# A transformer block on one core: another order for the first stretch, K in halves, V five beats later

## The reference

```python
def _tc_rmsnorm(x, t, gw, gb, bw, bb):
    g = (t @ gw.T + gb)[:, None, :]
    b = (t @ bw.T + bb)[:, None, :]
    return g * x * jax.lax.rsqrt(jnp.mean(x * x, axis=-1, keepdims=True) + EPS) + b

def _L0_cond_ref(x, t, ...):
    # 16 heads of 8 features; hidden width 512
    x = x + _attention(_tc_rmsnorm(x, t, g1w, g1b, b1w, b1b), Wq, Wk, Wv, Wo)
    return x + _swiglu(_tc_rmsnorm(x, t, g2w, g2b, b2w, b2b), gate_w, hid_w, out_w)

x = x + _L0_cond_ref(x, cond_256, ...)
```

## Time and profile before

| | us |
|---|---|
| median of the timed runs | 257.89 |
| the profiled execution | 257.42 |
| its span, first to last instruction | 255.6 |
| TensorE busy | 221.2 |
| VectorE busy | 202.9 |
| ScalarE busy | 163.3 |
| GpSimd busy | 111.9 |

### The profile page before, as it was taken

One profiled execution on the slowest core, in us unless ns is written; L12 is line 12 of the kernel. 1 busy time (PEld: TensorE's weight loads), 2 busy tenths in 40 slices (PEclk: granted clock), 3 DMA queues, 4 the chain that ended last, 5 costly groups with the idle time before them and its releaser, 6 DMA issues.

```text
span 255.6 us, 8235 instructions
## 1 busy us (share of the span) xinstructions
PE 221.2 (87%) x3048; PEld 177.9 (70%) x3048; DVE 202.9 (79%) x490; ACT 163.3 (64%) x352; POOL 111.9 (44%) x183
## 2 busy tenths in 40 slices
PE   2436777879989999899989999999999999899894
PEld 2314545547667868786878877887888778687894
DVE  4646966897899889889988998899888997565673
ACT  5354658676876686669766777567757655666430
POOL 8323852597265254625381516252623232323320
PEclk9995579999999999999999999999999999999998
DMA  5866601530261026100540045004500000000001
GB/s 162 345 169 147 185 4 28 152 85 3 64 166 27 26 64 164 47 23 19 140 124 0 27 112 152 10 27 114 156 6 26 4 26 3 23 3 24 22 21 44
DMA packets 18819, 18.79 MB, mean 74 GB/s; under 512 B 3644, under 2 KB 17980, under 8 KB 18652
## 3 DMA queue, kind: packets, MB, share of 16 engines
q1 hardware_dynamic: 18252, 17.80, 24.7%
q10 hardware_dynamic: 528, 0.46, 0.8%
HBM read 3.22 MB, written 2.10 MB: 21 GB/s over the span
## 4 chain that ended last, share of the span: by engine, by line
PE 45%; issue 24%; POOL 16%; DVE 9%; ACT 4%; ACTq 1%; POOLq 0%; DVEq 0%
PE proj L489 7%; PE pv L427 6%; PE ffn L320 5%; PE ffn L322 3%; PE ffn L321 3%; PE score L410 3%; DVE nmax L756 3%; POOL inv L923 3%; PE raw L383 3%; POOL qp L915 2%; PE tok L442 2%; POOL xn_lo L936 2%; POOL kp L915 2%; POOL xs L929 2%; PE proj L349 2%
## 5 line engine op out<-in xcount | busy, mean ns | idle before, releaser
L756 DVE TENSOR_REDUCE nmax<-raw 128x8 f32<-128x1024 f32 x61 | 74.2, 1216 | 3.0 <-PE raw L383 2.9
L597 ACT ACTIVATE p_s<-score 128x1024 f32<-128x1024 f32 x64 | 65.5, 1023 | 16.1 <-PE score L410 14.9
L427 PE MATMUL pv<-p_s,va 128*32 128x128 f32 x1024 | 41.7, 280 | 1.8 <-ACT xn L615 1.1
L320 PE MATMUL ffn<-xn_hi,ffn_hi 128*128 128x256 f32 x106 | 34.8, 328 | 1.2 <-POOL xn_lo L936 1.2
L626 ACT ACTIVATE th<-ffn 128x256 f32<-128x256 f32 x53 | 20.3, 384 | 19.6 <-PE ffn L322 19.6
L489 PE MATMUL proj<-ffn_out_s,hT 128*128 128x128 f32 x240 | 31.6, 275 | 0.0
L813 DVE SCALAR_TENSOR_TENSOR gated<-th,ffn 128x256 f32<-128x256 f32 x53 | 22.0, 415 | 12.1 <-ACT th L626 11.7
L427 PEld LDWEIGHTS pv<-p_s,va 128*32 128x32 f32 x1024 | 24.7, 109 | 9.2 <-issue 4.0
L936 POOL TENSOR_TENSOR xn_lo<-xn,xn_hi 128x128 fp32r<-128x128 f32 x32 | 14.7, 460 | 34.6 <-DVE xn_hi L804 34.6
L322 PE MATMUL ffn<-xn_hi,ffn_lo 128*128 128x256 f32 x106 | 29.7, 280 | 0.0
L321 PE MATMUL ffn<-xn_lo,ffn_hi 128*128 128x256 f32 x106 | 29.6, 279 | 0.0
(11 more groups left out here) (130 smaller groups left out, 456.0 us busy)
## 6 DMA issues: line engine op xcount, KB each, us to landing
ks<-kp SPq DMA_DIRECT2D x48, 128.0 KB, 2.4
qs<-qp SPq DMA_DIRECT2D x45, 128.0 KB, 2.5
out_y<-x_s SPq DMA_DIRECT2D x16, 128.0 KB, 1.8
x_s<-in_x SPq DMA_DIRECT2D x1, 1536.0 KB, 10.9
qs<-shift SPq DMA_DIRECT2D x64, 4.0 KB
x_s<-in_x SPq DMA_DIRECT2D x2, 256.0 KB, 3.6
ffn_in_s<-in_ffn_in_w SPq DMA_DIRECT2D x1, 512.0 KB, 6.7
qs<-qp ACTq DMA_DIRECT2D x3, 128.0 KB, 3.7
```

What stands on the lines that cost most here:

```text
L320: pe.matmul(dst, w_hi, v_hi, start=True, stop=False)
L427: mm = pe.matmul(pv[VW * j:VW * j + VW, (t % 2) * L:(t % 2 + 1) * L], va[vbuf(g)][:, t // 2, at:at + VW], p_s[:, (BEATS * g + t) % PBUF, p ...
L597: act.activation(p_s[:, n % PBUF, :], score[:], ACT.Exp, scale=SCALE).then_inc(s_exp, 1)
L756: dve.tensor_reduce(heads[:, :, t % 2, :], raw_dst(g, t)[:].rearrange("l (e j m) -> l e j m", e=HALVES, j=HQ), AX.X, ALU.max, negate=True) ...
```

## The change

- K of group 0 is computed in two halves of 256 columns (`first_key`), each behind its own half of `xn_lo`; `qk_lo` is made on GpSimd ahead of the second `a_inv`.
- On ScalarE the two last normalisations of group 1 stand ahead of the issue of the high queries' DMAs. The mean of group 2 and the zero fill of `va[1]` stand ahead of the middle part of Q of group 1.
- The cast to `ffn_hi` moves from beat 4 to the place behind `a_hi(1, 1)` on VectorE, and `ffn_lo` from beat 5 to behind `a_lo(1, 1)` on GpSimd.
- VectorE takes the first two maxima between the rests of K and Q of group 1. Six instead of seven raw scores stand ahead of beat 0; raw 6 and 7 come in beats 0 and 1, and raw 0 of group 1 at the end of beat 1. Only raw 1 and 3 use the bank `score`.
- V of group 0 moves behind the first score, and V of group g from beat 8g - 7 to 8g - 2. Its waits, and those of K and of the FFN's output, are adapted.
- `c_tr2` stands behind the next beat's `c_score` for beats below 10.

```diff
-    VALUE, KEY, QUERY = -7, -14, -13
+    VALUE, KEY, QUERY = -2, -14, -13
...
-            return score if g == 0 and t % 2 and t < BEATS - 1 else raw
+            return score if g == 0 and t % 2 and t < HQ else raw
...
+        def raws_in(T):
+            if T < 2:
+                return [(0, BEATS - 2 + T)]
+            return due(T, RAW, BEATS)
...                                       (a_values on TensorE)
-                elif g == 1:
-                    pe.wait_ge(s_va, 1)
                 else:
-                    pe.wait_ge(s_qrest, g + 1)
+                    pe.wait_ge(s_qrest, min(g + 2, G))
                 if g >= 3:
-                    pe.wait_ge(s_fin, WIN * (g - 3) + 1)
+                    pe.wait_ge(s_fin, WIN * (g - 3) + 2)
...                                       (a_key)
-                if g == 0:
-                    pe.wait_ge(s_wlo, 1)
-                elif g > 1:
-                    pe.wait_ge(s_va, g)
+                if g > 1:
+                    pe.wait_ge(s_va, g - 1)
+                if g > 3:
+                    pe.wait_ge(s_fin, WIN * (g - 4) + 1)
...
+            def first_key():
+                pe.wait_ge(s_wlo, 1)
+                for n in range(2):
+                    half = slice(2 * n * L, 2 * (n + 1) * L)
+                    pe.wait_ge(s_lo1, n + 1)
+                    mm = split_product(key_dst(0)[:, half], qk_hi[:, 1, :], qk_lo[:, 1, :], xn1_hi[:, half],
+                                       xn1_lo[:, half])
+                mm.then_inc(s_k, 1)
...                                       (c_score)
-                    pe.wait_ge(s_max, BEATS - 2)
+                    pe.wait_ge(s_max, HQ)
...                                       (d_out)
-                    pe.wait_ge(s_va, min(g + 3 + w, G))
+                    pe.wait_ge(s_va, min(g + 3, G))
...                                       (TensorE, first stretch and loop)
-            a_key(0)
+            first_key()
...
-            b_raw(0, 5)
             a_transpose(2, 0)
             a_transpose(2, 1)
-            a_values(0)
+            b_raw(0, 5)
             a_transpose(2, 2)
-            b_raw(0, 6)
             a_transpose(2, 3)
...
                     c_score(g, t)
-                for g, t in due(T, RAW, BEATS):
+                for g, i in due(T - 1, TR2, NB, 2):
+                    if T - 1 < FFN:
+                        c_tr2(g, i)
+                if T == 0:
+                    a_values(0)
+                for g, t in raws_in(T):
                     b_raw(g, t)
...
                     b_maxT(g, half)
+                if T == 1:
+                    b_raw(1, 0)
...
                 for g, i in due(T, TR2, NB, 2):
-                    c_tr2(g, i)
+                    if T >= FFN:
+                        c_tr2(g, i)
...                                       (ScalarE)
-            stack_high_queries()
             a_norm(1, 2)
             a_norm(1, 3)
+            stack_high_queries()
...
+            a_mean(2)
+            zero_fill(va[1][:].rearrange("l b v -> l (b v)"), s_va0[1])
             a_middle(1, s_qrest, q_rest, qp, s_qmid)
-            a_mean(2)
             a_mean(3)
...                                       (VectorE)
             a_hi(1, 1)
+            dve.wait_ge(s_ffnin, 16)
+            dve.tensor_copy(ffn_hi[:], ffn_in_s[:]).then_inc(s_whi, 1)
             zero_values(0)
             a_rest(1, key_dst(1), kp, k_rest, s_khi, s_klo, s_krest)
+            b_max(0, 0)
+            b_max(0, 1)
             a_rest(1, query_dst(1), qp, q_rest, s_qhi, s_qlo, s_qrest)
...                                       (GpSimd)
             a_inv(0)
-            a_inv(1)
             pool.wait_ge(s_whi, 1)
             pool.tensor_tensor(qk_lo[:], ...).then_inc(s_wlo, 1)
+            a_inv(1)
...
             a_lo(1, 1)
+            pool.wait_ge(s_whi, 2)
+            pool.tensor_tensor(ffn_lo[:], ...).then_inc(s_wlo, 1)
             a_lowest(1, k_rest, kp, s_kmid, s_klo)
+            a_inv(2)
+            a_scale(2)
             a_lowest(1, q_rest, qp, s_qmid, s_qlo)
```

More of the change, by code:

```diff
@@ L373, in b_raw @@
                         pe.wait_ge(s_xn1, 2 * NB)
-                    if t == BEATS - 1:
+                    if t > HQ:
                         pe.wait_ge(s_max, t)
@@ L668, in _ @@
             a_middle(1, s_krest, k_rest, kp, s_kmid)
+            a_mean(2)
+            zero_fill(va[1][:].rearrange("l b v -> l (b v)"), s_va0[1])
             a_middle(1, s_qrest, q_rest, qp, s_qmid)
-            a_mean(2)
             a_mean(3)
-            zero_fill(va[1][:].rearrange("l b v -> l (b v)"), s_va0[1])
-            a_norm(2, 0)
-            a_norm(2, 1)
-            a_values(0)
-            a_norm(2, 2)
-            a_norm(2, 3)
+            for b in range(NB):
+                a_norm(2, b)
             for T in range(LAST + 1):
@@ L851, in _ @@
             a_hi(1, 1)
+            dve.wait_ge(s_ffnin, 16)
+            dve.tensor_copy(ffn_hi[:], ffn_in_s[:]).then_inc(s_whi, 1)
             zero_values(0)
             a_rest(1, key_dst(1), kp, k_rest, s_khi, s_klo, s_krest)
+            b_max(0, 0)
+            b_max(0, 1)
             a_rest(1, query_dst(1), qp, q_rest, s_qhi, s_qlo, s_qrest)
-            for t in range(HQ):
-                b_max(0, t)
+            b_max(0, 2)
+            b_max(0, 3)
             b_shift(0, 0)
-            for t in range(HQ, BEATS - 1):
-                b_max(0, t)
+            b_max(0, 4)
+            b_max(0, 5)
             for T in range(LAST + 1):
@@ L874, in _ @@
                     b_shift(g, half)
-                if T == HQ:
-                    dve.wait_ge(s_ffnin, 16)
-                    dve.tensor_copy(ffn_hi[:], ffn_in_s[:]).then_inc(s_whi, 1)
+                if T == 1:
+                    b_max(1, 0)
                 for g, p in due(T, FFN, PIECES):
@@ L978, in _ @@
             a_lo(1, 1)
+            pool.wait_ge(s_whi, 2)
+            pool.tensor_tensor(ffn_lo[:], ffn_in_s[:], ffn_hi[:].bitcast(F32), ALU.subtract).then_inc(s_wlo, 1)
             a_lowest(1, k_rest, kp, s_kmid, s_klo)
+            a_inv(2)
+            a_scale(2)
             a_lowest(1, q_rest, qp, s_qmid, s_qlo)
             surround_values(0)
-            a_inv(2)
-            a_scale(2)
             a_inv(3)
@@ L1003, in _ @@
                     a_lo(g, 1)
-                if T == HQ + 1:
-                    pool.wait_ge(s_whi, 2)
-                    pool.tensor_tensor(ffn_lo[:], ffn_in_s[:], ffn_hi[:].bitcast(F32), ALU.subtract).then_inc(s_wlo, 1)
                 for g, _ in due(T, INV1, since=4):
```

## The result

The changed kernel takes 259.85 us (median of 7 runs, 259.62 to 260.25), the kernel before beside it 257.94 (7 runs, 257.65 to 258.99). The ratio is 1.0064, with a 95% interval of 1.0046 to 1.0083: slower by 0.6%, where I had forecast 257.6 and no change. The profiled execution took 259.68 us; its span is 257.8, against 255.6.

A forecast was written before the change was run, and what follows sets the result against it. It took TensorE's own work to bound beats 32 to 40 and waits to bound beats 0 to 10. 257.42 - 2.0 (lead at beat 10) + 2.2 (later V) = 257.6 us, no change; 8 in 10 range 255.0 to 259.6.

The forecast's parts named there:

- Part A: Up to the score of beat 0: it starts at 30.8, 2.0 us earlier (bounds 1.0 and 3.0).
- Part B: Beats 0 to 10: gains and losses leave a lead of 2.0 us at beat 10 (bounds 0.5 and 3.6).
- Sum at the score of beat 10: 2.0: Score of beat 10: 0.9 + 1.0 + 0.4 - 1.0 + 0.7 = 2.0 us earlier, at 59.2 in place of 61.23.
- the read-out wait: Score of beat 2: must wait for ScalarE to read out the transpose, 0.92 us from transpose to score.
- beat 3 keeps 0.9: Beats 2 to 3: the lead of 0.9 us at the score of beat 2 stays, as `xn_lo` of group 2 is no earlier.
- `c_tr2` behind the score takes the wait for `ot_s` out: Scores of beats 3, 5, 7, 9: takes a wait of 0.75 us off the chain; of four, 1.0 kept.
- The casts: Beats 4 to 7: moving `ffn_hi` and `ffn_lo` early frees 1.65 us on VectorE, of which 0.4 counted.
- V of group 2 leaves beat 9: Beat 9: the next score is held by the read-out, so 0.7 of 0.99 us is gained.
- rival 3: Early beats: without V of group 1 there, full clock comes only behind beat 4, about 2.0 us lost: 259.6; chance 0.09.
- Rival 2: Beats 0 and 1: VectorE idles as maxima wait, lead at beat 10 only 0.5 us: 259.1; chance 0.15.
- Part C: Groups 2 to 7, V from beat 8g - 7 to 8g - 2: costs 2.2 us together (bounds -0.9 and +4.0).
- 0.67 by group: V's new beat: one V costs 0.99 us less 0.32 of idle wait for `o_s`, so 0.67.

The follow-up runs named there:

- e1: Kernel before with only K of group 0 in halves, `qk_lo` early and two normalisations ahead of the high queries' DMAs: 255.85 us, ratio 0.9927.
- e3: Kernel before with only `c_tr2` behind the next score below beat 10: 257.93 us, ratio 0.9997.
- e8: e1 with the casts `ffn_hi` and `ffn_lo` made early, as in the change: 255.73 us, ratio 0.9920.
- e9: e1 with the change's order around beats 0 and 1 (V of group 0, raw 6 and 7 in one bank, raw 0 of group 1): 258.41 us.
- e14: e9 with added matmuls that keep TensorE busy in idle places: 255.82 us, ratio 0.9908.
- e6: e1 with added matmuls that keep TensorE busy, ahead of beat 0 and in beats 1 and 2: 255.03 us, ratio 0.9889.
- e2: Kernel before with only V of group g moved from beat 8g - 7 to 8g - 2: 260.18 us, ratio 1.0093.
- e5: Changed kernel with added matmuls, results unread, in TensorE's idle places ahead of beat 2: 256.91 us, ratio 0.9960.
- e15: Kernel before with the added matmuls of e6: 257.68 us, ratio 0.9984.
- e10: e6 with V of group g in beat 8g - 2 and three more added matmuls where V of group 1 stood: 255.64 us, ratio 0.9928.
- e13: e9 with V of group 0 back ahead of beat 0: 258.19 us, ratio 1.0012.

## Why the prediction was wrong

**Part A was right.** Beat 0 was put 2.0 earlier and came 1.71 earlier. Each step is in the trace: K of group 0 near 11.7, the first raw score at 21.75 (put at 21.8) behind a DMA, the first shift at 28.18. The early cast beside `xn_lo` cost 0.38 where I had 0.6, hidden by the same DMA. e1 shows the gain in timed runs: 1.9 us.

**Part B failed: "Sum at the score of beat 10: 2.0", measured -1.35.** The miss of 3.35 splits by beats.
- *0.3 up to beat 0*, the rest of part A.
- *0.85 in beats 0 and 1*: of the lead I gave back 1.1 there, and 1.95 was lost. I had V of group 0, raw 6, 7 and the read-out wait in the sum, with the right mechanism (the score of beat 2 does wait 0.59 behind its transpose). V took 2.0 and not 1.7, raw 7 began at 35.60, the last raw score of beat 1 at 37.94 and not 37, and the transpose at 38.48 and not 37.5. Part of this loss lies in what I compare with: the one execution of before that I read had the full clock in beats 0 and 1. Against before at the lower clock (the trace of e3) the lead at beat 2 is 0.65, near the 0.9 of the forecast.
- *0.6 in beat 2*: "beat 3 keeps 0.9". It lost more, because K, PV and the scores ran at the lower clock to 43 us. Beat 2 took 3.60 (3.01 before, 2.54 in e3).
- *1.6 from beat 3 to beat 10*: I had +1.1 and measured -0.5, all of it in beat 3. There, `c_norm` comes late: VectorE waits 2.11 for `tok` at 43.96, and TensorE then 0.81 for `oT_s` at 46.02. Beats 4 to 9 together last as long as before (15.43 and 15.44). The step "`c_tr2` behind the score takes the wait for `ot_s` out", counted as 1.0 of four times 0.75, shortens beat 4 (1.67, 2.31 before), and beat 5 is 0.46 longer. In beats 6 and 8 there was no such wait to take out: the idle time stood at `d_xt2`, 0.68 and 0.60 before and 0.68 and 0.68 after. e3 shows the price of the step: 0. The casts, counted as 0.4, are worth 0.1 (e8). That V of group 2 leaves beat 9 gives 0.39, not 0.7.

The term that the sum put at nothing is the clock. It carried the durations of the one trace of before over to a new order, and the change to the clock stood only in rival 3.

**Rival 2 and rival 3 both happened.** Rival 2 was to decide at maximum 7 of group 0 ending later than 37.2: it ended at 37.47. e9 against e1 and e14 against e6 show this mechanism, an extra maximum behind beat 0 and the waits on it, and its size: 1.7 and 1.8 at beat 2, at the lower clock and at the full one. Rival 3 had named the place (V of group 1 gone, TensorE waiting for VectorE) and the sign that came, with a price of 2.0. That the clock stays low to 44 us with late V alone is shown by e2. The sign given for it, a granted clock below 1.00 behind 39 us, did not come in the profile of after, because its clock column is wrong; the durations show it. The 2.9 of e5 is not its price. A low clock up to 39 us or later costs three of these kernels about 3 us against a full one: 2.9 from after to e5, 3.0 from e9 to e14 and 3.0 from e1 to e6 between the profiled executions. What the change seems to do is to make the low clock the rule. All seven runs of after lie within 259.6 to 260.3, while four of six of e1 are 1.1 shorter than the low-clock one, and of before the median is about 0.9 shorter than its runs at 258.5 to 259.0. So my estimate for the clock's share of the loss, from these times, is 0.9 of 1.9 us.

With like executions compared the parts also add up. From e1's long runs, 257.0, the order adds 1.8 and late V 1.4, which makes 260.2; measured 259.85.

My chance for rival 3, 0.09, was too small: the earlier trace rows show that the clock rose where V of group 1 kept TensorE busy, and no row spoke against the rival. TensorE: Matmul & The Clock Gate of the Trainium skill (section "Part 1: The HAM clock gate") says that the low clock is the default and that activity releases it; e5 and e14 agree in one direction and e2 in the other, while e15 shows a clock that fell in spite of added matmuls. The same section puts the cost of the ramp below 1% of a typical kernel and advises against fitting it to a count of slow matmuls; here it is 2.9 of 259.85 us in the changed kernel, 1.1%, and that is more than the whole difference between the two kernels.

**Part C: mechanism right, size wrong, 2.2 forecast and 0.85 measured.** Without V the beats 17, 25 and 33 last 3.03, 3.04 and 3.03 (3.44 before), as forecast from the read-out of the transpose. TensorE in beat 17 of after:

```profile
88.25 0.27 PE L340 MATMUL score<-ident,xs 128*128 128x128 f32 x1
88.36 0.39 PE L460 MATMUL tok<-attn_w_s,oT_s 128*128 128x128 f32 x2
89.17 0.40 PE L424 MATMUL score<-qs,ks 64*128 64x128 bf16 x8 [0.43 <-issue]
```

0.43 idle and 0.92 from transpose to score, the very figures of beat 13 in the earlier trace rows. The beats with V last 0.9 more (beats 22, 30, 38). What I mis-sized is what comes back behind them: behind beats 22 and 30 the next beat is 0.49 shorter (3.32 against 3.81), not 0.32. The term "0.67 by group" is the one that was too large, it measured 0.41:

| from beat | 10 to 16 | 16 to 24 | 24 to 32 | 32 to 40 | 40 to 48 | 48 to 56 |
|---|---|---|---|---|---|---|
| forecast | 0.67 | 0.35 | 0.27 | 0.32 | 0.50 | 0.10 |
| measured | 0.39 | 0.01 | 0.00 | 0.28 | 0.41 | -0.17 |

Beats 41 and 49, where no transpose stands, last 2.43 against 3.33 and so give all of V. But beat 42 takes 0.79 of it back, because K of group 7 waits for `xn_lo`, as I had it:

```profile
172.80 0.50 PE L326 MATMUL proj<-xn_hi,qk_hi 128*128 128x512 f32 x1 [0.39 <-POOL xn_lo L930]
```

Three pairs of traces agree on the sum from beat 10 to 56: 0.92 in after, 0.90 in e2, 0.91 in e10.

**What stays open.** Why the clock rises at one place in one execution and later in the next is not shown: up to beat 0 TensorE's work is the same in before and in e3, and behind 28 us it rose near 32 us in the one trace and near 41 in the other. The clock's share of 0.9 is worked out from how the runs group by recorded clock, not from a run that changed the clock alone. Of raw 6, raw 7 and their single bank I moved none alone, so the 1.8 of the order is not divided further, except that V of group 0 has 0.2 to 0.5 of it (e13).

## What to carry to other kernels

Before moving work out of a beat in which one engine is always busy, ask what the clock does there: if the granted clock rises behind it, the work may be worth more in its place than its own duration. Read more than one execution of the old kernel before taking durations from it, because one may have had the clock up where most have not. Before moving an instruction to escape a wait, find in the trace at which instruction the wait stands in each beat: here two of four stood at another. And try the parts of a change alone: three steps of this one were worth 1.9 us, and the rest cost about 4.
